# Part of the probabilities in three fp32r passes: a Perceiver layer on one Trainium2 core

## The chip, the core and the metric

The kernel runs on one core of a Trainium2 chip. The metric is the device time of one execution in microseconds (us). TensorE is PE in the profile (PEld its weight loads), VectorE is DVE, ScalarE is ACT, GpSimd is POOL and the DMA queues used are those of SyncE (SP).

## What is computed

One token set of 256 rows of 1024 (x) and a context of 4096 rows go through a cross attention, a linear attention and a mixture of low-rank experts, each with a residual:

```python
x = x + xattn(layernorm(x), ctx)   # 32 heads of 128, 4 key/value heads, keys = context and latents, 4352
x = x + attn(layernorm(x))         # 32 heads, decayed linear attention, RMS norm, sigmoid gate
x = x + ffn(layernorm(x))          # 4 experts of rank 16, top 2
# xattn:
q = latents @ Wq ; k, v = hidden @ Wk, hidden @ Wv
attn = softmax(q @ k.T / sqrt(128))
out = (attn @ v) @ Wo
```

All of it is float32.

## The kernel before

**Precision.** A float32 product is taken in one of two ways. In *three passes* (`three_pass`, line 110) each operand is split into a high part, rounded to fp32r, and a low part, the rest; hi·hi, hi·lo and lo·hi are three fp32r matmuls. *Plain*, a float32 matmul goes to TensorE as it is; the trace shows it as two records.

**Stages.** `project_keys_values` makes keys (high and low, in DRAM) and values (DRAM), and splits the query weights. `cross_attention` follows, then `project_out` with Wo, `linear_attention`, `project_out` again, and `lora_mixture`.

**Cross attention** (line 485) goes over 16 pairs of heads; a pair n is a *slot*, and 512 columns (two heads by 256 tokens). The 4352 keys are 17 double tiles j of 2 x 128. `slots` (line 546) writes the slots' order: slot 0, a loop over three groups of four slots, and three last ones. The key/value head changes every fourth slot, where u is 0. In a slot the engines run side by side, each by its own handwritten order, tied by semaphores:

- TensorE (`pe_slot`, line 903): for each j, the values matmul of pair n (`pe_values`, line 874: probabilities times v, two plain matmuls into `o_ps`), then the scores of pair n+1, two double tiles ahead (`pe_scores`, line 840, six fp32r matmuls). After the last j come the transposes of the maxima (`pe_peak`), the query projection of pair n+3 and the spreading of the maxima over partitions (`pe_spread`).
- VectorE (`dve_slot`, line 790): for each j, the row tile j+1 less the maximum (`dve_shift`, line 771), then the running maximum of pair n+1 (`dve_peak`, lines 746 to 759). In steps 4 to 7 four reciprocals for the previous pair are added (line 779).
- ScalarE (`act_slot`): exp of tile j+1 into one of three buffers of probabilities (`act_exp`, line 646), then the copy of the scores of pair n+1 out of PSUM (`act_row`, line 628).
- GpSimd (`pool_slot`, line 711): the probabilities of tile j are added into `sums` (line 696), 16 additions of 128x1024 a slot, then the two halves to each other (line 702), and in step 9 the previous pair's output is scaled (line 709).

There are three buffers of probabilities, so exp of tile j waits for the values matmul and the addition of tile j-3:

```python
back = j - KEEP
if back >= 0:
    act.wait_ge(pv_done, J * n + back + 1)
    if not last:
        act.wait_ge(added, (J - 1) * n + max(back, 1))
```

In the last slot there are no scores of a next pair. GpSimd adds the odd tiles and VectorE the even ones (line 788), into two tiles that are summed at the end (`pe_sums_last`, line 893). After step 11 VectorE also makes the low parts of the first step of the Wo projection (`Projection.low`, line 977).

**project_out** (line 986) takes 16 steps of two heads, with weights and inputs loaded two steps ahead; the wo instance also loads the first weights of linear attention, in four halves, between its own loads. Then comes a layer norm (`LayerNorm`, line 124): statistics and normalized rows per token tile, transposes by TensorE (line 182), a high part by ScalarE (line 189) and a low part by VectorE (line 195). While TensorE has nothing to do there it runs dummy matmuls (`keep_clock`, line 117), 8 and 10 before the two groups of transposes.

**linear_attention** (line 1221) goes over 16 pairs of heads. Of the two tiles of keys, the second is masked for the first 128 tokens; its scores and values are computed with all 256 columns, and four small tiles of zeros are set by GpSimd at the start.

Of the kernel before, what the change touches and what calls it, by code (L numbers as in the profile page):

```python
# [26 lines left out]
F32R = mybir.dt.float32r  # L27
# [6 lines left out]
KT = HIDDEN // P  # L34
TOK = 256
# [88 lines left out]
class LayerNorm:  # L124
# [53 lines left out]
    def pe_turn(self, pe, t):  # L178

        pe.wait_ge(self.h_ready, t + 1)  # L180
        for k in range(KT):
            last = pe.transpose(self.turned[:, k, t * P:(t + 1) * P], self.h[:, t, k * P:(k + 1) * P], self.ident[:, :])
            if t == QT - 1 and k % 2:
                last.then_inc(self.turned_ready, 1)

    def act_hi(self, act):
        for b in range(KT // 2):
            act.wait_ge(self.turned_ready, b + 1)
            act.activation(self.hT_hi[:, 2 * b:2 * b + 2, :], self.turned[:, 2 * b:2 * b + 2, :],
                           ACT.Copy).then_inc(self.hi_ready, 1)  # L190

    def dve_lo(self, dve):
        for b in range(KT // 2):
            dve.wait_ge(self.hi_ready, b + 1)
            dve.tensor_tensor(self.hT_lo[:, 2 * b:2 * b + 2, :], self.turned[:, 2 * b:2 * b + 2, :],
                              f32(self.hT_hi[:, 2 * b:2 * b + 2, :]), ALU.subtract).then_inc(self.lo_ready, 1)


def project_keys_values(nc, x, ctxT, wk, wv, wq, x_sb, hT_hi, hT_lo, ident, ones, k_drams, v_dram, wq_drams, shared):
# [5 lines left out]
    with ExitStack() as ctx:  # L205
        a = Alloc(nc, ctx, "kv_")
        w_raw = a.sb("w_raw", [P, KT, KVH * D])
# [14 lines left out]
                       k_ps[:, :, :].rearrange("p g (a n) -> p (g a) n", n=TOK), hT_hi, hT_lo, ident)  # L222
# [107 lines left out]
        def _(act):  # L330
# [19 lines left out]
            ln.act_hi(act)  # L350
# [31 lines left out]
        def _(dve):  # L382
# [28 lines left out]
            ln.dve_lo(dve)  # L411
# [25 lines left out]
        def _(pe):  # L437
# [26 lines left out]
            pe.wait_ge(ln.lo_ready, KT // 2)  # L464
# [6 lines left out]
LEAD = 2  # L471
KEEP = 3
# [7 lines left out]
def starts_piece(j):  # L480

    return j == 0 or j in ENDS


def cross_attention(nc, wq_drams, k_drams, v_dram, hT_hi, hT_lo, ident, ones, oT_dram, shared, proj, last_pair):
# [9 lines left out]
    with ExitStack() as ctx:  # L495
        a = Alloc(nc, ctx, "xa_")
        kT_hi, kT_lo = shared.r
        v = a.sb("v", [P, KV])
# [22 lines left out]
        v_in = [a.sem(f"v_in{i}") for i in range(len(ENDS))]  # L521
        q_done = a.sem("q_done")
# [100 lines left out]
        def act_row(act, n, b, j, first=False):  # L623

            act.wait_ge(peak_done, J * n + j + 1)
            if not first:
                act.wait_ge(exp_done, J * (n - 1) + j + 1)
            act.activation(rows[j], s_ps[:, 2 * b:2 * b + 2, :], ACT.Copy).then_inc(row_ready, 1)  # L628

        def act_exp(act, n, j, first=False, last=False):  # L630
# [3 lines left out]
            if back >= 0:  # L634
# [11 lines left out]
            act.activation(probs[j % KEEP], rows[j], ACT.Exp, scale=SCALE).then_inc(exp_done, 1)  # L646

# [49 lines left out]

        def pool_sum(pool, n, first):
# [12 lines left out]
        def pool_slot(pool, n, u, g, first=False, last=False):  # L711
            has_prev, has_next, has_query = flags(u, first, last)
            for j in range(1, J):
                if has_next:
                    pool_add(pool, n, j, not has_prev)
                elif j % 2:
# [4 lines left out]
                    else:  # L721
                        pool.wait_ge(added, (J - 1) * n + j // 2)
# [49 lines left out]

        def dve_inverse(dve, n, c):
# [7 lines left out]
        def dve_add_last(dve, n, j):  # L781

            dve.wait_ge(exp_done, J * n + j + 1)
            if j == 2:
                dve.tensor_copy(peak[:, :, :], probs[j % KEEP]).then_inc(added_last, 1)
            else:
                dve.wait_ge(added_last, j // 2 - 1)
                dve.tensor_tensor(peak[:, :, :], peak[:, :, :], probs[j % KEEP], ALU.add).then_inc(added_last, 1)

        def dve_slot(dve, n, u, g, first=False, last=False):  # L790
            has_prev, has_next, has_query = flags(u, first, last)
            for j in range(J):
                if j + 1 < J:
                    dve_shift(dve, n, j + 1)
                if has_next:
                    dve_peak(dve, n + 1, (u + 1 + j) % 2, j)
                if not has_next and j >= 2 and j % 2 == 0:
# [7 lines left out]
                if not has_next and j == 11:  # L805
# [68 lines left out]
        def pe_values(pe, n, j, values, first):  # L874
# [3 lines left out]
            if values is not None and starts_piece(j):  # L878
                pe.wait_ge(v_in[piece_of(j)], 16 * (values + 1))
            pe.wait_ge(exp_done, J * n + j + 1)  # L880
            for t in range(2):
                at = slice((2 * j + t) * P, (2 * j + t + 1) * P)
                last = pe.matmul(o_ps[:, :], v[:, at], probs[j % KEEP][:, t, :], start=j == 0 and t == 0,  # L883
# [9 lines left out]
        def pe_sums_last(pe):  # L893

            pe.wait_ge(inverse_ready, 4 * LAST + 4)
            pe.wait_ge(added, (J - 1) * LAST + J // 2)
            pe.wait_ge(added_last, J // 2)
# [5 lines left out]
        def pe_slot(pe, n, u, g, first=False, last=False):  # L903
# [7 lines left out]
            for j in range(J):  # L911
                pe_values(pe, n, j, values, not has_prev)
# [31 lines left out]
FIRST_QUARTER = 6  # L944

# [40 lines left out]
def project_out(nc, name, proj, x_sb, h, hT_hi, hT_lo, ident, stores, prefetch, prefetches,  # L986
                norm=None, meanwhile=None, quarters=None, last_pair=None):
# [4 lines left out]
    with ExitStack() as ctx:  # L992
        a = Alloc(nc, ctx, name)
        y_ps = a.ps("y_ps", [P, QT, 2, BANK])
        turned = a.ps("turned", [P, KT, TOK])
# [6 lines left out]
        summed = a.sem("summed")  # L1002
        small = a.sem("small")
        root_ready = a.sem("root_ready")
# [32 lines left out]
        def _(act):  # L1037
# [19 lines left out]
            ln.act_hi(act)  # L1057

        @block.vector
        def _(dve):  # L1060
            proj.low(dve, 1, 1)
            if norm is not None:
                dve.wait_ge(summed, 1)
                dve.tensor_scalar(ve[:, :], turned[:, 0, 0:QT], 1.0 / (HEADS * D), EPS, ALU.mult, ALU.add).then_inc(small, 1)
# [24 lines left out]
            if norm is not None:  # L1089
                dve.wait_ge(small, 6)  # L1090
            for t in range(QT):
                for half in range(2):
# [10 lines left out]
                    if t > 0 and half == 0:  # L1103
# [691 lines left out]
```

## Time and profile before

| | |
|---|---|
| median of 3 runs | 2023.38 us (2022.89 to 2028.67) |
| profiled execution | 2030.37 us, span 2028.5 us |
| mean granted TensorE clock | 0.991 |
| PE busy | 1987.3 us, 98% of the span |
| DVE busy | 1245.9 us, 61% |
| ACT busy | 947.0 us, 47% |
| POOL busy | 776.0 us, 38% |
| cross attention, slots | from about 441 to 1388 us |
| linear attention | 1490 to about 1905 us |

The span is the time from the first to the last instruction; the execution's own time is 1.9 us longer. Busy shares are means over stages with different limits. Weight loads overlap matmuls. A matmul's length in a row includes its way through the array, so the distance between starts, and not the length, is what one costs in a stream.

### The profile page before, as it was taken

The page shows a single profiled execution, that of the slowest core. Times are in us where ns is not written, and L with a number is a line of the kernel's source. Part 1 is how long each engine was busy: PE and PEld are TensorE (multiplying, and loading weights), DVE is VectorE, ACT ScalarE, POOL GpSimd, SP SyncE. Part 2 cuts the span into 40 slices and gives each one's busy share as a digit, 9 for nine tenths or more (in the row PEclk, how much of TensorE's full clock was granted, in tenths as well). Part 3 has the DMA queues.
Part 4 walks back from the last instruction along what each step waited for, and adds up shares of the span by engine and source line. Part 5 has one row for each costly group of instructions (what it writes and reads, how often), then busy time and mean ns, then how long its engine had stood idle before and what let it go on. Part 6 is the DMA issues. An engine that isn't in the chain of part 4 may idle for free. (4 is left out here: it accounts for less than half of the span.)

```text
span 2028.5 us, 27101 instructions
## 1 busy us (share of the span) xinstructions
PE 1987.3 (98%) x9797; PEld 1534.1 (76%) x9797; DVE 1245.9 (61%) x1298; ACT 947.0 (47%) x1000; POOL 776.0 (38%) x345
## 2 busy tenths in 40 slices
PE   9999999999999999999999999998999999999998
PEld 7878888876666666566666666655889999999886
DVE  4312221267877767877677877887756666666555
ACT  3112110155665555665565665654634544445442
POOL 2444320026776666766566766762000000000200
PEclk9999999999999999999999999999999999999998
DMA  8788873420032110321112210015735554444461
GB/s 305 297 310 328 323 280 145 174 93 35 13 109 94 65 48 15 112 92 60 43 47 94 78 60 1 6 57 177 278 136 186 186 184 179 176 176 169 157 233 73
DMA packets 72224, 283.85 MB, mean 140 GB/s; under 512 B 6400, under 2 KB 24320, under 8 KB 56512
## 3 DMA queue, kind: packets, MB, share of 16 engines
q1 hardware_dynamic: 72128, 282.65, 38.1%
q8 instruction: 51, 0.84, 0.2%
q14 instruction: 45, 0.37, 0.1%
HBM read 212.89 MB, written 69.73 MB: 139 GB/s over the span
## 5 line engine op out<-in xcount | busy, mean ns | idle before, releaser
L696 POOL TENSOR_TENSOR xa_sums<-xa_sums,stage 128x1024 f32<-128x1024 f32 x150 | 358.4, 2389 | 117.8 <-ACT stage L646 113.5
L883 PE MATMUL xa_o_ps<-stage,xa_v 128*128 128x512 f32 x768 | 362.3, 595 | 5.4 <-ACT stage L646 5.4
L750 DVE TENSOR_TENSOR xa_peak<-xa_s_ps,xa_peak 128x1024 f32<-128x1024 f32 x224 | 274.1, 1223 | 107.0 <-PE xa_s_ps L114 107.0
L112 PE MATMUL xa_s_ps<-xa_qT_hi,split 128*128 128x512 f32 x544 | 306.9, 564 | 6.6 <-issue 3.9
L628 ACT ACTIVATE xa_rows<-xa_s_ps 128x1024 f32<-128x1024 f32 x208 | 213.4, 1026 | 123.5 <-DVE xa_peak L750 107.4
L771 DVE TENSOR_TENSOR xa_rows<-xa_rows,xa_r_ps 128x1024 f32<-128x1024 f32 x208 | 248.4, 1195 | 0.0
L883 PEld LDWEIGHTS xa_o_ps<-stage,xa_v 128*128 128x128 f32 x768 | 144.2, 190 | 124.3 <-issue 106.2
L114 PE MATMUL xa_s_ps<-xa_qT_hi,split 128*128 128x512 f32 x544 | 215.6, 396 | 0.0
L696 POOL TENSOR_TENSOR xa_sums<-xa_sums,xa_probs 128x1024 f32<-128x1024 f32 x75 | 179.2, 2389 | 91.3 <-ACT xa_probs L646 89.8
L113 PE MATMUL xa_s_ps<-xa_qT_lo,split 128*128 128x512 f32 x544 | 213.5, 392 | 0.0
L646 ACT ACTIVATE stage<-xa_rows 128x1024 f32<-128x1024 f32 x144 | 152.4, 1058 | 100.0 <-DVE xa_rows L771 97.5
L1396 DVE TENSOR_TENSOR pair_lo<-pair_raw,pair_hi 128x4096 fp32r<-128x4096 f32 x30 | 132.8, 4426 | 81.3 <-ACT pair_hi L1333 81.3
L1323 POOL TENSOR_TENSOR square_sum<-square_sum,la_squares 128x512 f32<-128x512 f32 x16 | 20.7, 1295 | 387.5 <-ACT la_squares L1363 387.5
L112 PEld LDWEIGHTS xa_s_ps<-xa_qT_hi,split 128*128 128x128 f32 x544 | 103.2, 190 | 77.2 <-issue 55.8
L373 DVE TENSOR_TENSOR kv_k_lo<-kv_k_ps,kv_k_hi 128x512 fp32r<-128x512 f32 (+1 forms) x36 | 23.5, 660 | 222.2 <-ACT kv_k_hi L321 222.2
L321 ACT ACTIVATE kv_k_hi<-kv_k_ps 128x512 fp32r<-128x512 f32 (+1 forms) x36 | 20.3, 571 | 288.0 <-DMA kT_lo_scratch<-kv_k_lo 228.2
L113 PEld LDWEIGHTS xa_s_ps<-xa_qT_lo,split 128*128 128x128 f32 x544 | 103.4, 190 | 66.9 <-issue 53.6
L883 PE MATMUL xa_o_ps<-xa_probs,xa_v 128*128 128x512 f32 x320 | 150.5, 592 | 1.7 <-ACT xa_probs L646 1.7
L112 PE MATMUL la_qk_ps<-hT_hi,pair_hi 128*128 128x256 f32 x512 | 145.0, 283 | 0.7 <-PEq L992 0.7
L113 PE MATMUL la_qk_ps<-hT_lo,pair_hi 128*128 128x256 f32 x512 | 144.9, 283 | 0.0
L114 PE MATMUL la_qk_ps<-hT_hi,pair_lo 128*128 128x256 f32 x512 | 144.9, 283 | 0.0
L693 POOL TENSOR_TENSOR xa_sums<-stage 128x1024 f32<-128x1024 f32 x15 | 35.9, 2393 | 250.5 <-ACT stage L646 250.5
(301 smaller groups left out, 4672.2 us busy)
## 6 DMA issues: line engine op xcount, KB each, us to landing
pair_raw<-in_w_qk SPq DMA_DIRECT2D x15, 2048.0 KB, 7.7
pair_raw<-in_w_gv SPq DMA_DIRECT2D x15, 2048.0 KB, 7.6
kv_w_raw<-in_wq SPq DMA_DIRECT2D x16, 1024.0 KB, 7.9
wq_hi_scratch<-x_hT_hi SPq DMA_DIRECT2D x16, 1024.0 KB, 4.3
wq_lo_scratch<-x_hT_lo SPq DMA_DIRECT2D x16, 1024.0 KB, 5.0
full<-in_wo SPq DMA_DIRECT2D x16, 1024.0 KB, 5.2
pair_raw<-in_w_out SPq DMA_DIRECT2D x16, 1024.0 KB, 5.0
xa_w_hi<-wq_hi_scratch SPq DMA_DIRECT2D x15, 1024.0 KB, 4.8
```

The source lines that it names most:

```text
L112: pe.matmul(out, w_hi, m_hi, start=first, stop=False)
L113: pe.matmul(out, w_hi, m_lo, start=False, stop=False)
L114: return pe.matmul(out, w_lo, m_hi, start=False, stop=last)
L373: dve.tensor_tensor(k_lo[:, g % 2, 0:n], k_ps[:, g, 0:n], f32(k_hi[:, g % 2, 0:n]), ALU.subtract).then_inc(k_copied, 1)
L628: act.activation(rows[j], s_ps[:, 2 * b:2 * b + 2, :], ACT.Copy).then_inc(row_ready, 1)
L646: act.activation(probs[j % KEEP], rows[j], ACT.Exp, scale=SCALE).then_inc(exp_done, 1)
L693: pool.tensor_tensor(sums[:, :, :], probs[0], probs[1], ALU.add).then_inc(added, 1)
L696: pool.tensor_tensor(sums[:, :, :], sums[:, :, :], probs[j % KEEP], ALU.add).then_inc(added, 1)
L750: dve.tensor_tensor(peak[:, :, :], s_ps[:, 2 * b:2 * b + 2, :], peak[:, :, :], ALU.max).then_inc(peak_done, 1)
L771: dve.tensor_tensor(rows[j], rows[j], r_ps[:, :].unsqueeze(1).to_broadcast([P, 2, W]), ALU.subtract).then_inc(shifted, 1)
L883: last = pe.matmul(o_ps[:, :], v[:, at], probs[j % KEEP][:, t, :], start=j == 0 and t == 0, stop=j == J - 1 and t == 1)
L1396: dve.tensor_tensor(w_lo[part][:, :, :], raw[part][:, :, :], f32(w_hi[part][:, :, :]), ALU.subtract).then_inc(w_lo_ready[part], 1)
```

## The change

Five of the 17 double tiles (j = 2, 5, 8, 11, 14) have their values product in three passes, in all slots but the last. For them ScalarE writes exp a second time, rounded to fp32r (`probs_hi`), and the low part is `probs - probs_hi`: by GpSimd right after its addition for j = 2, 8, 14, by VectorE for j = 5, 11, between the shift of tile j+1 and the maximum. The values of these tiles are split once per key/value head, in slots with u = 0 (ScalarE high, VectorE low, 128x256 each). The last slot is all plain, with the unsplit values of the five tiles loaded into the query weights' buffer; its additions go 12 to GpSimd and 4 to VectorE, and the low parts of the first Wo step come after the last tile. Values are loaded in 12 pieces instead of 4.

To make room, `x_sb` lives only from the Wo projection on and x is loaded twice. Layer norms turn and split one token tile after the other, the last parts of the out projection are reordered so that token tile 0 is complete earlier, and the dummy matmuls are 1 and 13. In linear attention the masked half of the second key tile is left out: 128 columns instead of 256, and no zeros are set.

```diff
+SPLIT_STEPS = (2, 5, 8, 11, 14)
+LOW_BY_VECTOR = (5, 11)
+LAST_BY_VECTOR = (4, 8, 12, 16)
...
             act.activation(probs[j % KEEP], rows[j], ACT.Exp, scale=SCALE).then_inc(exp_done, 1)
+            if j in SPLIT_STEPS and not last:
+                act.activation(probs_hi[:, :, :], rows[j], ACT.Exp, scale=SCALE).then_inc(probs_hi_ready, 1)
...
+                if u == 0 and j + 2 in SPLIT_STEPS:
+                    act_values(act, g, j + 2)
...
+        def pool_low(pool, n, j):
+
+            pool.wait_ge(exp_done, J * n + j + 1)
+            pool.wait_ge(probs_hi_ready, SPLIT * n + SPLIT_STEPS.index(j) + 1)
+            pool.tensor_tensor(probs_lo[:, :, :], probs[j % KEEP], f32(probs_hi[:, :, :]), ALU.subtract).then_inc(low_by_pool, 1)
...
                 if has_next:
                     pool_add(pool, n, j, not has_prev)
+                    if j in LOW_BY_POOL:
+                        pool_low(pool, n, j)
...
                 if j + 1 < J:
                     dve_shift(dve, n, j + 1)
+                if has_next and j in LOW_BY_VECTOR:
+                    dve_low(dve, n, j)
                 if has_next:
                     dve_peak(dve, n + 1, (u + 1 + j) % 2, j)
+                if u == 0 and j + 2 in SPLIT_STEPS:
+                    dve_values(dve, g, j + 2)
...
-                if not has_next and j == 11:
+                if not has_next and j == J - 1:
                     proj.low(dve, 0, 0)
...
+            if j in SPLIT_STEPS and not last_slot:
+                if values is not None:
+                    pe.wait_ge(v_lo_ready, SPLIT * values + SPLIT_STEPS.index(j) + 1)
+                if j in LOW_BY_VECTOR:
+                    pe.wait_ge(low_by_vector, len(LOW_BY_VECTOR) * n + LOW_BY_VECTOR.index(j) + 1)
+                else:
+                    pe.wait_ge(low_by_pool, len(LOW_BY_POOL) * n + LOW_BY_POOL.index(j) + 1)
+                for t in range(2):
+                    at = slice(split_columns(j).start + t * P, split_columns(j).start + (t + 1) * P)
+                    last = three_pass(pe, o_ps[:, :], v_hi[:, at], v_lo[:, at], probs_hi[:, t, :], probs_lo[:, t, :],
+                                      False, False)
...
+LAST_PARTS = ((0, 0, 0), (0, 0, 1), (0, 1, 0), (1, 0, 0), (1, 0, 1), (0, 1, 1), (1, 1, 0), (1, 1, 1))
...
-            for t, count in zip(range(QT), (8, 10)):
+            for t, count in zip(range(QT), (1, 13)):
...
-                    last = three_pass(pe, a_ps[:, h, jt, :], qk_hi[:, h, 1, key], qk_lo[:, h, 1, key],
-                                      qk_hi[:, h, 0, :], qk_lo[:, h, 0, :], True, True)
+                    at = slice(jt * P, TOK)
+                    last = three_pass(pe, a_ps[:, h, jt, at], qk_hi[:, h, 1, key], qk_lo[:, h, 1, key],
+                                      qk_hi[:, h, 0, at], qk_lo[:, h, 0, at], True, True)
...
         def load_first_pair(sp, i):
+            if i == 3:
+                sp.dma_start(x_sb[:, :, :], x).then_inc(x_in, 16)
             weights.load_half(sp, i // 2, i % 2)
```

## Rows read from the trace of the kernel before

**Rows 1.** Stretches: us, PE, PEld, DVE, ACT, POOL busy, clock, DMA share, GB/s.
```profile
808.38:869.09 60.71, 60.71 (x235) 39.36 (x234) 46.74 (x43) 36.40 (x36) 40.70 (x19) 1.00 0.33 113
1346.20:1388.10 41.90, 34.82 (x81) 14.65 (x80) 38.02 (x32) 20.76 (x21) 21.65 (x9) 0.96 0.19 69
1490.00:1895.00 405.00, 405.00 (x3376) 405.00 (x3376) 242.31 (x274) 197.44 (x216) 20.33 (x20) 1.00 0.49 179
```

**Rows 2.** Timeline of TensorE, one step: start us, us, engine, line, what.
```profile
811.13 1.88 PE L883 MATMUL xa_o_ps<-stage,xa_v 128*128 128x512 f32 x4
813.08 0.40 PE L113 MATMUL xa_s_ps<-xa_qT_lo,split 128*128 128x512 f32 x1
814.24 1.88 PE L883 MATMUL xa_o_ps<-stage,xa_v 128*128 128x512 f32 x4
```

**Rows 3.** GpSimd and TensorE at tile 2; GpSimd subtractions at L982 (min/median/max ns).
```profile
813.65 2.39 POOL L696 TENSOR_TENSOR xa_sums<-xa_sums,xa_probs 128x1024 f32<-128x1024 f32 x1 [4.02 <-ACT xa_probs L646]
816.12 4.86 POOL L696 TENSOR_TENSOR xa_sums<-xa_sums,stage 128x1024 f32<-128x1024 f32 x2
817.34 1.88 PE L883 MATMUL xa_o_ps<-xa_probs,xa_v 128*128 128x512 f32 x4
L982 POOL TENSOR_TENSOR pair_hi<-pair_raw,pair_hi x2: 2399/2402/2406, 1896.6 to 1899.0; 128x1024 fp32r<-128x1024 f32 x2
```

**Rows 4.** ScalarE and TensorE: exp and values of tile 8.
```profile
830.98 1.06 ACT L646 ACTIVATE xa_probs<-xa_rows 128x1024 f32<-128x1024 f32 x1 [0.99 <-DVE xa_rows L771]
836.81 1.88 PE L883 MATMUL xa_o_ps<-xa_probs,xa_v 128*128 128x512 f32 x4
```

**Rows 5.** VectorE in steps 6 and 7 of the same slot.
```profile
827.70 1.22 DVE L750 TENSOR_TENSOR xa_peak<-xa_s_ps,xa_peak 128x1024 f32<-128x1024 f32 x1
828.85 0.95 DVE L779 RECIPROCAL xa_inverse<-xa_t_ps 128x128 f32<-128x128 f32 x1
829.71 1.16 DVE L771 TENSOR_TENSOR xa_rows<-xa_rows,xa_r_ps 128x1024 f32<-128x1024 f32 x1
```

**Rows 6.** VectorE and GpSimd, last slot; lines 982 and 753 (min/median/max ns).
```profile
1373.62 4.50 DVE L982 TENSOR_TENSOR split<-full,split 128x1024 fp32r<-128x1024 f32 x2
1374.13 2.90 POOL L723 TENSOR_TENSOR xa_sums<-xa_sums,xa_probs 128x1024 f32<-128x1024 f32 x1 [1.03 <-ACT xa_probs L646]
L982 DVE TENSOR_TENSOR split<-full,split x16: 1211/1223/3362, 1373.6 to 1466.3; 128x1024 fp32r<-128x1024 f32 x16
L753 DVE TENSOR_TENSOR xa_peak<-xa_peak x16: 692/2254/2259, 426.8 to 1338.1; 128x512 f32<-128x512 f32 x16
```

**Rows 7.** Last slot: GpSimd's first addition and TensorE's closing sums.
```profile
1351.40 2.35 POOL L720 TENSOR_TENSOR xa_sums<-stage 128x1024 f32<-128x1024 f32 x1 [5.20 <-ACT stage L646]
1387.96 1.45 PE L900 MATMUL xa_t_ps<-xa_sums,ones 128*128 128x512 f32 x3
```

**Rows 8.** TensorE: transposes in the first stage, then the spreading of the maxima.
```profile
345.87 1.91 PE L182 MATMUL kv_k_ps<-ident,kv_w_raw 128*128 128x128 f32 x16
347.53 0.48 PE L112 MATMUL kv_v_ps<-kv_wv_hi,kv_c_hi 128*128 128x512 f32 x1
863.17 1.05 PE L870 MATMUL xa_r_ps<-ident,xa_max_q 128*128 128x128 f32 x8
863.98 0.36 PE L112 MATMUL xa_q_ps<-x_hT_hi,xa_w_hi 128*128 128x256 f32 x1
```

**Rows 9.** Timeline of the tail after the first out projection.
```profile
1479.68 1.98 PE L121 MATMUL wo_y_ps<-wo_odd 128*128 128x512 f32 x8
1487.01 2.48 DVE L195 TENSOR_TENSOR hT_lo<-wo_turned,hT_hi 128x512 fp32r<-128x512 f32 x4 [1.16 <-ACT hT_hi L189]
1489.81 0.36 PE L112 MATMUL la_qk_ps<-hT_hi,pair_hi 128*128 128x256 f32 x1 [0.73 <-PEq L992]
```

**Rows 10.** Busy time by stretch: the first out projection, ten us.
```profile
1430.00:1440.00 10.00, 10.00 (x45) 8.27 (x45) 7.50 (x8) 6.96 (x8) 0.00 (x0) 1.00 0.95 356
```

More of the change, by code:

```diff
@@ L34 @@
 KT = HIDDEN // P
+HALF = KT // 2
 TOK = 256
@@ L349, in _ @@
             act.wait_ge(wq_stored, 32 * (PAIRS + 1))
-            ln.act_hi(act)
+            for t in range(QT):
+                ln.act_hi(act, t)
             copy_keys(act, NCHUNK, TOK)
@@ L410, in _ @@
             copy_values(dve, NCHUNK - 1, 1)
-            ln.dve_lo(dve)
+            for t in range(QT):
+                ln.dve_lo(dve, t)
             copy_values(dve, NCHUNK - 1, VT, 1)
@@ L471 @@
 LEAD = 2
+LAST_BY_VECTOR = (4, 8, 12, 16)
+LAST_BY_POOL = tuple(j for j in range(1, J) if j not in LAST_BY_VECTOR)
+SPLIT_STEPS = (2, 5, 8, 11, 14)
+LOW_BY_VECTOR = (5, 11)
+LOW_BY_POOL = tuple(j for j in SPLIT_STEPS if j not in LOW_BY_VECTOR)
+SPLIT = len(SPLIT_STEPS)
 KEEP = 3
@@ L482, in starts_piece, with plain_columns, split_columns, value_runs @@
     return j == 0 or j in ENDS
+def plain_columns(j0, j1):
+    back = sum(s < j0 for s in SPLIT_STEPS)
+    return slice(2 * P * (j0 - back), 2 * P * (j1 - back))
+def split_columns(j):
+    i = SPLIT_STEPS.index(j)
+    return slice(2 * P * i, 2 * P * (i + 1))
+def value_runs(i):
+    runs, start = [], ENDS[i - 1] if i else 0
+    for j in range(start, ENDS[i]):
+        if j in SPLIT_STEPS:
+            if start < j:
+                runs.append((start, j))
+            runs.append((j, j + 1))
+            start = j + 1
+    if start < ENDS[i]:
+        runs.append((start, ENDS[i]))
+    return runs
 def cross_attention(nc, wq_drams, k_drams, v_dram, hT_hi, hT_lo, ident, ones, oT_dram, shared, proj, last_pair):
@@ L584, in sync_slot @@
                 load_weight(sp, n + 3)
+            if last and u == 2:
+                sp.wait_ge(q_done, PAIRS)
+                load_last_values(sp)
             if not has_next:
@@ L872, in pe_spread, with pe_values @@
             last.then_inc(spread, 1)
-        def pe_values(pe, n, j, values, first):
+        def pe_values(pe, n, j, values, first, last_slot):
             if j == 0 and not first:
@@ L911, in pe_slot @@
             for j in range(J):
-                pe_values(pe, n, j, values, not has_prev)
+                pe_values(pe, n, j, values, not has_prev, not has_next)
                 if has_next and j + LEAD < J:
@@ L1001, in project_out @@
         r0 = a.sb("r0", [P, QT])
-        summed = a.sem("summed")
-        small = a.sem("small")
-        root_ready = a.sem("root_ready")
+        if norm is not None:
+            summed = a.sem("summed")
+            small = a.sem("small")
+            root_ready = a.sem("root_ready")
         mm_done = a.sem("mm_done")
@@ L1090, in _ @@
                 dve.wait_ge(small, 6)
+            if x_in is not None:
+                dve.wait_ge(x_in, 16)
             for t in range(QT):
@@ L1102, in _ @@
                     ln.dve_stats(dve, t, half)
-                    if t > 0 and half == 0:
-                        ln.dve_rows(dve, t - 1)
                 ln.dve_variance(dve, t)
-            ln.dve_rows(dve, QT - 1)
-            ln.dve_lo(dve)
+                ln.dve_rows(dve, t)
+            for t in range(QT):
+                ln.dve_lo(dve, t)
         def part(pe, par, h, t, b, first, last):
@@ L1128, in _ @@
                     for h in range(2):
-                        last = pe.matmul(turned[:, 0, t:t + 1], square_sum[:, h, t * P:(t + 1) * P], ones[:, 0:1],
+                        last = pe.matmul(turned[:, 0, 0, t:t + 1], square_sum[:, h, t * P:(t + 1) * P], ones[:, 0:1],
                                          start=h == 0, stop=h == 1)
```

143 lines of the change are left out of this document (91 added, 52 removed).

## The prediction

> **What bounds the kernel now.** I read the busy time by stretch first. In one slot of cross attention (808.38 to 869.09, the fifteen slots with a successor repeat it) TensorE is busy 60.71 of 60.71 us with the granted clock at full (2.4 GHz), while VectorE has 46.74, ScalarE 36.40 and GpSimd 40.70 us of work. The last slot, 41.90 us, is the one stretch of this part where TensorE has gaps. Linear attention, 405.00 us, is TensorE without a gap too [rows 1]. Then the timeline of TensorE inside the slot: a step is 811.13 to 814.24, 3.11 us. The second scores matmul starts at 813.08 and one such matmul is 0.23 us, so the plain values of a double tile take 811.13 to 812.85, 1.72 us, and the six fp32r scores matmuls 1.39 us [rows 2]. Third, the clearance between an exp and the values that use it, on the timelines of ScalarE, GpSimd and TensorE [rows 3, 4]; what a faster TensorE would collide with stands there.
>
> **The gain that is bought.** Six fp32r matmuls of 128x512 in place of four plain records: 1.72 - 1.39 = 0.33 us per split tile [rows 2], 1.65 us per slot, 75 tiles, 24.8 us in all, if nothing waits. ScalarE gets a second exp of 1.06 us five times a slot (5.3 us on top of 36.4): no bound by itself.
>
> **Tile 2.** GpSimd's addition of it starts at 813.65, released by its exp, and GpSimd's next instruction at 816.12, that and its successor lasting 4.86: back to back these are 2.44 us apart [rows 3]. The next one is now the subtraction, of the shape of the GpSimd fp32r subtraction of 128x1024, 2.40 us [rows 3]. It ends at about 818.5, and TensorE wants tile 2 at 817.34 [rows 3]. That exp hangs on the slot's first scores, so nothing moves it forward: TensorE waits 1.3 us with the hand-over, in each of fifteen slots.
>
> **Tile 8.** Its exp runs from 830.98 to 832.04 and TensorE takes it at 836.81: 4.8 us clear [rows 4]. Addition plus subtraction want 2 x 2.44 = 4.9 us, with hand-overs a wait of 0.3 us already with nothing late. But it will be late. In steps 4 to 7 VectorE runs peak, reciprocal and shift back to back: 827.70, 828.85, 829.71, next peak 3.1 us after the first, all of TensorE's step [rows 5]. The subtraction of tile 5 (1.22 us) is put there.
>
> It also meets the thing I take as this change's main price: a VectorE instruction with both inputs in SBUF and a GpSimd instruction don't run together. In the last slot two subtractions of 1.22 us each last 4.50 us from 1373.62, and GpSimd's addition from 1374.13 lasts 2.90 instead of 2.39: first it waits for VectorE's first one, then VectorE's second waits for it. The 128x512 maximum of two SBUF halves at line 753 takes 0.69 us at best and 2.25 in the median of the 16 slots [rows 6]. Instructions with one input in PSUM (the peak, the shift) keep their time beside GpSimd [rows 5]. The Trainium skill says the same (SBUF, State Buffer, "Who interferes with whom": a VectorE instruction with two SBUF inputs contends with a GpSimd instruction that reads SBUF, and one is fully blocked); by that rule the trace agrees. So tile 5's subtraction waits 1.1 us for an addition that is under way, takes 1.2, and GpSimd's next addition starts some 0.9 us later.
>
> Walking it through, in time from the slot's start (808.38): TensorE takes tile 2 at 10.25, not 8.96, and ends scores 4 at 13.0. VectorE does peak 4 from 13.2 (1.14 us), reciprocal (0.86) and shift 6 (1.13) to 16.3. GpSimd has ended tile 2's subtraction at 10.1 and adds tiles 3, 4, 5 until 17.45; tile 5's subtraction on VectorE waits for that and ends at 18.6. Peak 5, reciprocal, shift 7 (3.13), peak 6, reciprocal (2.0): shift 8 starts at 23.75, before at 829.71 - 808.38 = 21.3 [rows 5]. Exp 8 ends 2.4 us after it (1.27 to its start, as 829.71 to 830.98, and 1.06), 26.15; its addition runs 26.3 to 28.7, its subtraction to 31.15. TensorE could have taken tile 8 at 29.1 (28.43 before, +1.3, -0.66). It waits 2.15 us.
>
> **Tile 14.** From 26.3 on GpSimd does not rest: seven additions (8 to 14), two subtractions, the output of the previous pair (1.25), and VectorE's blocking instructions between them (tile 11, 1.2; line 753, 0.6): 9 x 2.44 + 3.05 = 25.0, so the low part of tile 14 is there at 51.3. TensorE would want it at 49.3: another 2.05 us.
>
> **Sum per slot:** waits 1.3 + 2.15 + 2.05 = 5.5, gain 1.65, net +3.85. Fourteen slots make +53.9; the first has no reciprocals and no output, so I give it +1.5. Bounds: above, GpSimd's two idle stretches (2.2 and 0.7 us before additions 7 and 8 in this walk) are in it already, so little more than +5. Below, without those stretches and without any blocking: GpSimd's chain from tile 2 to 14 is 16 x 2.44 + 1.25 = 40.3 from 5.27, tile 14 at 45.6, before TensorE needs it, and only tile 2 and 0.3 at tile 8 are left: 1.6 - 1.65 = -0.05.
>
> **Values split once per four slots.** Five small VectorE subtractions of 128x256 (about 0.35 us, from 1.22 for 1024) with both inputs in SBUF: each may wait up to 2.4 us for GpSimd, most of them where VectorE has 0.7 us a step to spare. I take +1.3 in each of four slots, +5 (0 to +12).
>
> **Last slot.** All plain. Additions go 12 to GpSimd, 4 to VectorE (before 8 and 8), and they exclude each other: 12 x 2.43 + 4 x 1.2 + 1.3 = 35.3 us from 1351.40 [rows 7]. That ends at 1386.7, where the closing sums start at 1387.96 now [rows 7]. The wo subtractions no longer hold a shift (that wait is gone), but the additions take its place. -0.5 (-4 to +3).
>
> **Linear attention.** 192 matmuls go from 256 to 128 columns. At 256 one takes 405.00/3376 = 0.120 us [rows 1]. No row has fp32r with 128. Lower end: half the columns off, 0.120 - 0.053 = 0.067, so -10. Upper end: a plain fp32 product of 128 columns is two records, eight of them from 863.17 to 863.98, so 0.20 us and +16 [rows 8]. Nearest: transposes of 128x128, each with its own weights, 16 from 345.87 to 347.53, 0.104 us each [rows 8]; I take that, -3. The Trainium skill (TensorE: Matmul & The Clock Gate, "LDWEIGHTS (loading the stationary operand)") gives a load as its columns over 1.2 GHz, 107 ns for 128; by it the term would be -2.5, and by the sustained 81 ns of "Back-to-back issue gap" -7.5. The four memsets that go were on idle GpSimd: 0.
>
> **Layer norms.** After each out projection the tail is 1479.68 to 1489.81, 10.1 us, and the last of it four low pieces, 2.48 us [rows 9]. With token tile 0 turned and split first only two pieces are left (-1.2), and the reordered last parts let tile 1's row start about 0.3 us earlier: -1.5 each, two tails, -3 (-5 to 0). The dummies before the transposes, 1 and 13 instead of 8 and 10, fill the same gap. In the first stage the turned tiles are covered by value matmuls: 0. The second load of x, 1 MB, (3 us at 356 GB/s) joins DMA engines that are 0.95 busy, but TensorE is busy 10.00 of 10.00 us there [rows 10]: 0 (to +3). Eight more load issues of values on SP's queue lie beside a whole slot: 0.
>
> **Total:** 53.9 + 1.5 + 5 - 0.5 - 3 - 3 = +53.9. The profiled execution took 2030.4 us (span 2028.5), so 2084; the median of the runs is 2023.4, and 2023.4 + 53.9 = 2077.
>
> **Rivals.**
> (A) Faster: GpSimd keeps up. The place is the pair of waits at tiles 8 and 14. For it speaks that GpSimd has 20 us free in a slot and that exp 8 led by 4.8 us [rows 1, 4]; against it the full VectorE steps and the blocking [rows 5, 6]. It decides when the waits of a slot stay under 1.65 us. With tile 2 alone waiting: 15 x -0.35 = -5, last slot, linear attention and norms -6.5, split values +1: -11, 2012.
> (B) The light version: blocking delays only a little, tile 8 waits 0.9, tile 14 0.6, net +1.15 a slot: +17 - 1.5 = 2039.
> (C) Narrow fp32r falls to the plain price: forecast + 19, 2096.
> (D) The waits come to 1.75 us a slot, +1.5 in all, against the other terms' -1.5: 2023, no change.
> (E) That the five tiles would stay plain in effect: outside the last slot the code sends all five through three passes, so this gets no chance.
>
> **How the numbers follow.** Forecast 0.60, (B) 0.16, (C) 0.08, (A) 0.10, (D) 0.06. A change under 0.3%, 6 us, can't be told from none here. Slower 0.84, same 0.06, faster 0.10. The range goes from (B)'s lower side, 2032, to between the forecast's upper bounds and (C), 2099.
>
> **What the profile after would show.** Right: the low-part subtraction on GpSimd about 2.4 us, TensorE idle before the fp32r values of tiles 2, 8 and 14, released by GpSimd, some 75 to 80 us in all; slots near 64.5 us; VectorE's subtraction at tiles 5 and 11 lasting over 2 us in the mean. Wrong: slots at or under 60.7 us, GpSimd with rests after tile 8, or TensorE released by ScalarE instead.

## The result, and the profile after

| | before | after |
|---|---|---|
| median | 2025.22 us (4 runs, 2022.89 to 2028.67) | 2084.59 us (4 runs, 2082.53 to 2096.87) |
| profiled execution, span | 2030.37, 2028.5 us | 2082.53, 2080.8 us |
| ratio | | 1.030, 95% interval 1.027 to 1.034: slower |

The page of the changed kernel, busy time of the engines:

```profile
PE 1970.9 (95%) x9939; PEld 1548.3 (74%) x9939; DVE 1305.4 (63%) x1344; ACT 1010.7 (49%) x1095; POOL 918.4 (44%) x390
```

Between the medians the change costs 59.4 us, between the two profiled executions 52.2 us; the stretches below are of these two executions.

TensorE is busy 16 us less than before, and its share falls from 98 to 95%: it has less to do and waits. The busy time by stretch (us, PE, PEld, DVE, ACT, POOL busy, clock, DMA share, GB/s) of an ordinary slot, two slots with u = 0 (the longest and another), the last slot and linear attention, in the changed kernel:

```profile
891.05:954.59 63.54, 59.92 (x244) 40.88 (x243) 48.70 (x45) 40.49 (x42) 49.57 (x22) 1.00 0.24 82
690.56:762.12 71.56, 63.14 (x243) 42.41 (x243) 57.27 (x50) 41.31 (x47) 48.83 (x22) 0.95 0.12 43
1215.39:1283.33 67.94, 60.41 (x244) 40.72 (x243) 55.39 (x50) 41.10 (x47) 49.48 (x22) 1.00 0.13 45
1405.84:1451.79 45.95, 39.66 (x96) 17.15 (x95) 36.15 (x29) 22.82 (x25) 32.89 (x15) 0.96 0.18 63
1548.79:1960.65 411.86, 411.23 (x3445) 411.06 (x3445) 248.07 (x283) 202.37 (x225) 26.05 (x19) 1.00 0.49 179
```

The first row stands against the 60.71 us of [rows 1], in which TensorE had no gap. Slots are cut here at the four transposes of the maxima, which stand once in each; the kernel before cut in the same way gives the middle column (differences of start times on the timelines of TensorE):

| stretch | before | after | difference |
|---|---|---|---|
| up to the first transposes of maxima | 431.07 | 431.61 | +0.54 |
| eight slots with u = 1, 2 or 3 | 60.67 to 60.72 | 63.54 to 63.61 | +2.84 to +2.94 each |
| four slots with u = 0 | 61.29, 60.70, 60.70, 60.70 | 68.18, 71.56, 67.90, 67.94 | +6.89, +10.86, +7.20, +7.24 |
| two slots after a turn of the loop | 64.40, 64.70 | 65.38, 65.78 | +0.98, +1.08 |
| all 15 to the last transposes | 913.48 | 974.23 | +60.75 |
| last slot, to the first Wo matmul | 47.94 | 45.95 | -1.99 |
| Wo projection and its norm | 97.32 | 97.00 | -0.32 |
| linear attention, to its last product | 414.13 | 411.86 | -2.27 |
| second projection and norm | 107.08 | 105.35 | -1.73 |
| mixture, to the end | 17.48 | 14.80 | -2.68 |

(The slot of 58.96 us that closes the 15, against 55.41, projects no query; it is the one not listed, +3.55.) The loss is wholly in the slots. What TensorE waits for there, from the waits of the changed kernel (total us, times, longest):

```profile
PE xa_o_ps L113 <- POOL xa_probs_lo L777: 56.9, 45, 1.8
PE xa_s_ps L113 <- ACT xa_rows L693: 14.3, 8, 3.2
```

The first is three tiles in 15 slots. One ordinary slot on the timeline of TensorE (start us, us, engine, line, what, idle before): the values of tiles 2, 8 and 14, and the matmul ahead of the last wait.

```profile
909.95 0.50 PE L113 MATMUL xa_o_ps<-xa_probs_hi,xa_v_hi 128*128 128x512 f32 x1 [0.94 <-POOL xa_probs_lo L777]
...
930.51 0.50 PE L113 MATMUL xa_o_ps<-xa_probs_hi,xa_v_hi 128*128 128x512 f32 x1 [1.37 <-POOL xa_probs_lo L777]
...
948.28 0.40 PE L115 MATMUL xa_s_ps<-xa_qT_hi,split 128*128 128x512 f32 x1
949.99 0.50 PE L113 MATMUL xa_o_ps<-xa_probs_hi,xa_v_hi 128*128 128x512 f32 x1 [1.31 <-POOL xa_probs_lo L777]
950.33 0.40 PE L114 MATMUL xa_o_ps<-xa_probs_lo,xa_v_hi 128*128 128x512 f32 x1
```

A stall costs more than its idle time: matmuls in a stream start 0.23 us apart, so the one at 949.99 could have started at 948.51, 1.48 us earlier and not 1.31, and the next one follows it after 0.34 us. That is 1.6 us for 1.31 shown, so about 0.29 us more at each stall.

GpSimd in the same slot, from tile 2 to tile 14, and VectorE's subtraction of tile 5:

```profile
905.16 2.38 POOL L771 TENSOR_TENSOR xa_sums<-xa_sums,xa_probs 128x1024 f32<-128x1024 f32 x1 [4.02 <-ACT xa_probs L711]
907.51 2.38 POOL L777 TENSOR_TENSOR xa_probs_lo<-xa_probs,xa_probs_hi 128x1024 fp32r<-128x1024 f32 x1
909.86 4.85 POOL L771 TENSOR_TENSOR xa_sums<-xa_sums,stage 128x1024 f32<-128x1024 f32 x2
...
916.08 2.18 DVE L860 TENSOR_TENSOR xa_probs_lo<-xa_probs,xa_probs_hi 128x1024 fp32r<-128x1024 f32 x1
917.49 3.05 POOL L771 TENSOR_TENSOR xa_sums<-xa_sums,stage 128x1024 f32<-128x1024 f32 x1 [0.32 <-ACT stage L711]
...
925.74 2.37 POOL L771 TENSOR_TENSOR xa_sums<-xa_sums,xa_probs 128x1024 f32<-128x1024 f32 x1 [0.69 <-ACT xa_probs L711]
928.08 2.37 POOL L777 TENSOR_TENSOR xa_probs_lo<-xa_probs,xa_probs_hi 128x1024 fp32r<-128x1024 f32 x1
...
936.49 3.25 POOL L771 TENSOR_TENSOR xa_sums<-xa_sums,xa_probs 128x1024 f32<-128x1024 f32 x1
...
947.10 2.84 POOL L777 TENSOR_TENSOR xa_probs_lo<-xa_probs,xa_probs_hi 128x1024 fp32r<-128x1024 f32 x1
```

The low part comes behind the addition at 905.16 and 925.74, and from 925.74 to 949.9 no row carries a wait: 24.2 us without rest. The addition of 3.05 us is held by VectorE's subtraction of tile 5, that of 3.25 by tile 11's (from 935.83, 1.67 us), and the low part of 2.84 us starts beside the 128x512 maximum of two SBUF halves (946.87). VectorE's subtractions by line (860 probabilities, 866 values; min/median/max ns):

```profile
L860 DVE TENSOR_TENSOR xa_probs_lo<-xa_probs,xa_probs_hi x30: 1266/1800/2536, 457.6 to 1386.9; 128x1024 fp32r<-128x1024 f32 x30
L866 DVE TENSOR_TENSOR xa_v_lo<-xa_v_lo,xa_v_hi x20: 412/1988/2483, 443.1 to 1269.8; 128x256 fp32r<-128x256 f32 x20
```

The second row is the one I had not taken seriously enough. Where it happens, step 6 of the slot with u = 0 that takes 71.56 us (VectorE, GpSimd and ScalarE):

```profile
723.30 2.38 POOL L771 TENSOR_TENSOR xa_sums<-xa_sums,stage 128x1024 f32<-128x1024 f32 x1 [2.15 <-ACT stage L711]
...
723.48 2.48 DVE L866 TENSOR_TENSOR xa_v_lo<-xa_v_lo,xa_v_hi 128x256 fp32r<-128x256 f32 x1 [0.38 <-ACT xa_v_hi L719]
...
725.88 0.94 DVE L874 RECIPROCAL xa_inverse<-xa_t_ps 128x128 f32<-128x128 f32 x1
...
728.02 1.06 ACT L711 ACTIVATE xa_probs<-xa_rows 128x1024 f32<-128x1024 f32 x1 [3.66 <-DVE xa_rows L854]
...
730.98 0.50 PE L113 MATMUL xa_s_ps<-xa_qT_hi,split 128*128 128x512 f32 x1 [3.20 <-ACT xa_rows L693]
```

A subtraction of 128x256 starts 0.18 us behind a GpSimd addition and ends with it, 2.48 us later, in a step in which VectorE has nothing to spare. All maxima, shifts and exps behind it move back. ScalarE makes the copy of the scores after the exp in its order, so the copy is late too, and in the end TensorE waits 3.20 us for it: a wait of another name than the 45, in none of my terms.

The slot is 3.6 us longer than the two like it (67.90 and 67.94 us), and that is the clock. All three have this wait, 3.20, 3.19 and 3.20 us; their mean granted clocks are 0.95, 0.97 and 1.00. Behind the wait at 730.98 TensorE ran at 1.2 GHz: the fp32r matmuls from 735.02 to 738.86 start 0.43 us apart instead of 0.23 (granted clock 0.53 from 732 to 739 us). VectorE's shifts lie at the same places of this slot and of the one of 67.94 us up to 46 us after its start, and 3.6 us later at its end.

### The profile page after: what moved, and what is told of

Its sections match the earlier page's. It is cut to its first block and busy times, and to the rows that moved or that the text cites. A ratio compares the mean times of both kernels' runs of the same rounds, so it can differ in the third digit from the quotient of the medians.

```text
span 2080.8 us, 27859 instructions
## 1 busy us (share of the span) xinstructions
PE 1970.9 (95%) x9939; PEld 1548.3 (74%) x9939; DVE 1305.4 (63%) x1344; ACT 1010.7 (49%) x1095; POOL 918.4 (44%) x390
## 5 line engine op out<-in xcount | busy, mean ns | idle before, releaser
L771 POOL TENSOR_TENSOR xa_sums<-xa_sums,stage 128x1024 f32<-128x1024 f32 x150 | 368.3, 2455 | 45.0 <-ACT stage L711 39.5
L113 PE MATMUL xa_s_ps<-xa_qT_hi,split 128*128 128x512 f32 x544 | 269.5, 495 | 20.0 <-ACT xa_rows L693 14.3
L771 POOL TENSOR_TENSOR xa_sums<-xa_sums,xa_probs 128x1024 f32<-128x1024 f32 x75 | 190.0, 2533 | 88.7 <-ACT xa_probs L711 85.2
L115 PE MATMUL xa_s_ps<-xa_qT_hi,split 128*128 128x512 f32 x544 | 214.6, 394 | 0.0
L1440 POOL TENSOR_TENSOR square_sum<-square_sum,la_squares 128x512 f32<-128x512 f32 x16 | 20.8, 1301 | 385.7 <-ACT la_squares L1480 385.7
L113 PEld LDWEIGHTS xa_s_ps<-xa_qT_hi,split 128*128 128x128 f32 x544 | 102.7, 189 | 89.6 <-ACT xa_rows L693 34.9
L115 PEld LDWEIGHTS xa_s_ps<-xa_qT_hi,split 128*128 128x128 f32 x544 | 102.6, 189 | 23.4
```

The lines of the kernel that those rows point to most:

```text
L113: pe.matmul(out, w_hi, m_hi, start=first, stop=False)
L115: return pe.matmul(out, w_lo, m_hi, start=False, stop=last)
L771: pool.tensor_tensor(sums[:, :, :], sums[:, :, :], probs[j % KEEP], ALU.add).then_inc(added, 1)
```

## Experiments

Each is an edit of the changed kernel unless it says otherwise. The time of before beside them was 2024.8 to 2026.7 us.

**1. No tile split.**

```diff
-SPLIT_STEPS = (2, 5, 8, 11, 14)
-LOW_BY_VECTOR = (5, 11)
+SPLIT_STEPS = ()
+LOW_BY_VECTOR = ()
```

> The changed kernel with no tile in three passes (the list of split tiles is empty; no second exp, no low parts, no split values), all its other parts kept: last slot 12 to 4, layer norms, 128 columns in linear attention, second load of x. Theory: the whole loss is in the slots. TensorE's maxima transposes lie 60.75 us further apart from the first to the last in the changed kernel than before, and everything outside gives about -8.5 us; so the slots go back to 60.70 us and the time is about 2016 us (2013 to 2020), ratio to before 0.9955. Rival: one of the other parts costs something that the slots hide (the second load of x, the reordered last parts), and the time is 2022 us or more.

2018.5 us (6 runs), ratio 0.9965 (0.9953 to 0.9977). An ordinary slot, by stretch:

```profile
858.82:919.54 60.72, 60.72 (x234) 39.37 (x233) 46.74 (x43) 36.43 (x37) 40.68 (x19) 1.00 0.24 86
```

The ordinary slots are those of before, and the other parts together gain some 7 us. All of the loss is the splitting.

**2. The values' subtraction with an input from PSUM.** VectorE has an instruction of the same size, on other numbers: the values' low parts are not computed.

```diff
-            dve.tensor_tensor(v_lo[:, at], f32(v_lo[:, at]), f32(v_hi[:, at]), ALU.subtract)
+            dve.tensor_tensor(v_lo[:, at], f32(v_lo[:, at]), r_ps[:, 0:2 * P], ALU.subtract)
```

> The changed kernel, but VectorE's subtraction for the values of a split tile (128x256) takes its second input from a tile in PSUM instead of the high part in SBUF; same size, same waits, so the values' low parts are not the right ones. Theory (blocking): in the slots with u = 0 this instruction took 1.75 us in the mean instead of 0.35 because GpSimd was adding, and that cost these four slots 4.0 to 8.0 us each beyond the others, some 21 us in all; with one input in PSUM they fall to within 1 us of the other slots (63.6): about 2066 us (2063 to 2072), ratio to the changed kernel 0.991. Rival (the work itself, ScalarE's copies and the twelve loads delay these slots): less than 4 us saved, 2081 us or more.

2067.9 us (4 runs), ratio to before 1.0207 (1.0190 to 1.0224), 16.7 us less than the changed kernel. By line and form the instruction is now

```profile
L866 DVE TENSOR_TENSOR xa_v_lo<-xa_v_lo,xa_r_ps 128x256 fp32r<-128x256 f32 x20 | 8.4, 419 | 5.8 <-ACT xa_v_hi L719 5.8
```

419 ns in place of 1751. The slots with u = 0 are 65.05, 64.70, 64.72 and 64.69 us, the others as they were (63.6). With an instruction of the same size, 1.1 us a slot is left of the 4 to 8. The blocking made the rest: 3.2 us in three of the slots and 6.9 in the one of 71.56, where 3.6 of them are the fall of the clock behind the wait, which is not there in this run.

**3. The same for VectorE's low parts of tiles 5 and 11**, which are then not computed either.

```diff
-            dve.tensor_tensor(probs_lo[:, :, :], probs[j % KEEP], f32(probs_hi[:, :, :]), ALU.subtract)
+            dve.tensor_tensor(probs_lo[:, :, :], probs[j % KEEP], r_ps[:, :].unsqueeze(1).to_broadcast([P, 2, W]),
+                              ALU.subtract)
```

> The changed kernel, but VectorE's low parts of tiles 5 and 11 (128x1024) take their second input from PSUM (the spread maxima) instead of the high part; same size and waits, so these low parts are not the right ones. Theory (blocking): the subtraction of tile 5 falls from 2.18 to 1.22 us, shift and exp of tile 8 come 0.96 us earlier and TensorE's wait at tile 8 falls from 1.37 to 0.4; GpSimd's addition beside tile 11's subtraction falls from 3.25 to 2.4 us and the wait at tile 14 from 1.31 to about 0.45. 1.8 us a slot, about 2057 us (2050 to 2064). Rival (GpSimd's amount of work sets both waits, not the blocking): the slots stay over 63 us and the time over 2077 us.

2048.5 us (4 runs), ratio to before 1.0120 (1.0104 to 1.0137). The instruction by line, and tile 8 on TensorE:

```profile
L860 DVE TENSOR_TENSOR xa_probs_lo<-xa_probs,xa_r_ps x30: 1203/1209/1216, 457.2 to 1350.6; 128x1024 fp32r<-128x1024 f32 x30
909.93 0.50 PE L113 MATMUL xa_o_ps<-xa_probs_hi,xa_v_hi 128*128 128x512 f32 x1 [0.61 <-POOL xa_probs_lo L777]
```

Ordinary slots are 61.3 us, 2.2 less (I had 1.8): the wait at tile 8 falls from 1.37 to 0.61, at tile 14 it is gone, at tile 2 it stays 0.94. The slots with u = 0 are still 66.0 us (the first 67.4). What VectorE's subtraction loses to GpSimd counts twice, once as a later exp 8 and once as a longer addition in GpSimd's own list. The time is 1.5 us under the range that I gave.

**4. The low part before the addition** on GpSimd, nothing left out.

```diff
-                    pool_add(pool, n, j, not has_prev)
                     if j in LOW_BY_POOL:
                         pool_low(pool, n, j)
+                    pool_add(pool, n, j, not has_prev)
```

> The changed kernel, but GpSimd makes the low part of tiles 2, 8 and 14 before it adds the tile. Theory (backlog): the waits at tiles 2 and 8 go, since the low part comes up to 2.4 us earlier, but GpSimd still runs back to back from exp 8 to tile 14 (24.3 us in the changed kernel, less the addition of 14 = 21.9 us, and now it starts a second exp later), so its low part comes about 47.5 us after the slot's first values, TensorE wants it at 45.6, and tile 14 still waits 1.5 to 2 us: slots near 61 us, about 2045 us (2038 to 2050). Rival (only the order at each tile matters): all three waits go, the slots are 60.70 - 1.85 = 58.85 us and the time is 2014 to 2022 us.

2028.1 us (10 runs), ratio to before 1.0014 (1.0005 to 1.0023): 56 us for the exchange of two instructions. GpSimd at tiles 8 and 14:

```profile
895.08 2.40 POOL L777 TENSOR_TENSOR xa_probs_lo<-xa_probs,xa_probs_hi 128x1024 fp32r<-128x1024 f32 x1 [1.14 <-ACT xa_probs_hi L713]
897.43 2.43 POOL L771 TENSOR_TENSOR xa_sums<-xa_sums,xa_probs 128x1024 f32<-128x1024 f32 x1
...
914.30 2.83 POOL L777 TENSOR_TENSOR xa_probs_lo<-xa_probs,xa_probs_hi 128x1024 fp32r<-128x1024 f32 x1
```

The ordinary slots are 60.80 us and TensorE waits at tile 14 alone, 1.4 to 1.5 us: the mechanism and the slot are the theory's. The time, 10 us under my range, is not, since I forgot the slots with u = 0 in the sum: with the slack won they fall from some 68 (one 71.56) to 62.3 us (the first to 62.9), and VectorE's values subtraction from 1751 to 743 ns in the mean.

**5. The stretch from exp 8 to tile 14 made shorter**: experiment 4, with the scaling of the output behind tile 14's low part.

```diff
-                if has_prev and j == 9:
+                if has_prev and j == (15 if has_next else 9):
                     pool_output(pool, n - 1, 1 - u % 2, 8 * (n - u % 2) + 16)
```

> The kernel with the low part ahead of the addition on GpSimd (only tile 14 waits, a stall of 1.75 us a slot), with the scaling of the previous pair's output (1.3 us on GpSimd) moved from step 9 to step 15, behind tile 14's low part; complete. Theory (between exp 8 and tile 14 GpSimd does not rest, so each microsecond taken from that stretch comes off the wait): the stall falls to about 0.45 us, the slots to 59.5 us in 14 slots, 2010 us (2006 to 2015). Rival (the wait hangs on exp 14 and not on GpSimd's list): no change, 2026 to 2030 us. A later output also holds the store and the key and value loads behind it on SP's queue; if these were needed sooner, the slots with a new key/value head would be longer by over 2 us.

2009.1 us (4 runs), ratio 0.9923 (0.9902 to 0.9944). No wait at tile 14 is left: 1.73 us went with its hand-over, for 1.3 us of GpSimd's work. Ordinary slots are 59.40 us, only 1.40 less, because 0.33 us is lost in a new place. The scores behind tile 11's values wait for their copy, and two matmuls there start 0.43 and 0.34 us after the one before them instead of 0.23; VectorE's subtraction of tile 11 just ahead takes 2.99 us.

**6. Tile 14 not split**, with experiment 4 (`SPLIT_STEPS = (2, 5, 8, 11)`).

> GpSimd's low part ahead of its addition, and tile 14 not split: four split tiles (2, 5, 8, 11); complete. Theory (backlog): the wait at tile 14 is gone with nothing in its place, the slots are 60.70 - 4 x 0.37 = 59.2 us, 2004 us (2000 to 2009). Rival (the wait came from something ahead of tile 14, and goes to an exp near it): slots at 60.5 us or more, 2020 us or more.

2005.5 us (4 runs), ratio 0.9903 (0.9888 to 0.9918). Ordinary slots 59.40 us, no wait for a low part.

**7. Tile 14's low part by VectorE**, with experiment 4 (`LOW_BY_VECTOR = (5, 11, 14)`).

> The changed kernel with GpSimd's low part ahead of its addition, and tile 14's low part given to VectorE (as tiles 5 and 11 have it); complete. In the run with the low part first, only the wait at tile 14 was left (1.45 us and its hand-over) and the slots were 60.80 us. Theory (GpSimd's backlog from exp 8 to tile 14 is the last cost): one low part less and no one waiting for it, no wait is left, the slots are 60.70 - 5 x 0.37 = 58.85 us, 1999 us (1995 to 2005), faster than the kernel before. Rival (VectorE's third subtraction, near 1.8 us with the blocking, delays the last maxima or the rows of the slot's end): slots at 60 us or more, 2015 us or more.

2012.1 us (6 runs), ratio 0.9938 (0.9921 to 0.9954). Ordinary slots are 59.03 to 59.31 us, near the theory's, but the slots with u = 0 are 62.8 us (the first 63.7): there TensorE waits 0.97 and 0.6 us for rows and 1.2 us for the last maxima. The rival's mechanism was right in these slots, and I had again left them out of the sum; the time lies between the two ranges.

**8. As 7, with the values' low parts on GpSimd too.**

```diff
+                    if u == 0 and j + 1 in SPLIT_STEPS:
+                        pool_values(pool, g, j + 1)
                     pool_add(pool, n, j, not has_prev)
...
-                if u == 0 and j + 2 in SPLIT_STEPS:
-                    dve_values(dve, g, j + 2)
```

> As the kernel with the low part first and tile 14 on VectorE, but GpSimd also makes the low parts of the values (128x256, ahead of its addition, one step before the tile), so VectorE has none; complete. Theory (blocking of VectorE in its full steps is what the slots with u = 0 paid): their 1.5 us each beyond the others go, another 4 to 6 us off, 1994 us (1990 to 2000). Rival (GpSimd has no room for them in its backlog, or the loads bind): no change or slower than the kernel without this.

2001.9 us (5 runs, 1999.4 to 2005.3), ratio 0.9884 (0.9868 to 0.9899), 10 us less than 7. The time is 1.9 us over my range. The slots with u = 0 are 60.9 us and not 59.1; in three of them 1.1 us is a wait for the last maxima. An ordinary one, by stretch:

```profile
849.71:908.78 59.07, 59.07 (x244) 41.08 (x243) 50.09 (x46) 40.19 (x42) 48.59 (x21) 1.00 0.26 88
```

TensorE has no gap again, and a slot is 60.70 - 59.07 = 1.63 us shorter than before. This kernel leaves nothing out and takes 1.2% less time than the kernel before.

**9. As 6, with the values' low parts on GpSimd.**

> Four split tiles (2, 5, 8, 11), the low part ahead of the addition, and the low parts of the values on GpSimd; complete. Theory: the slots with u = 0 (60.78 us with the values' low parts on VectorE, the others 59.40) come to within 0.5 us of the others, 2001 us (1997 to 2005), so the fifth tile is worth little. Rival (GpSimd's four additional instructions bring back a wait at tile 11 or 8 in these slots): 2005 us or more.

2003.6 us (4 runs), ratio 0.9898 (0.9881 to 0.9915). The slots with u = 0 are 59.99 us, the others 59.4 to 59.5. It can't be told from 8: the fifth tile's 0.33 us a slot is about what it costs in the slots with u = 0.

**10. No tile split, 8 and 10 dummies.**

```diff
-            for t, count in zip(range(QT), (1, 13)):
+            for t, count in zip(range(QT), (8, 10)):
```

> The kernel without split tiles, with 8 and 10 dummy matmuls around the transposes of the layer norms as before, instead of 1 and 13. Before, the granted clock was 0.50 for the first 5 us of the mixture stage; in the changed kernel it is 1.00 there and this stage is 2.4 us shorter. Theory (the shorter gap ahead of it, from turning and splitting one token tile after the other): the clock stays at 1.00 there, the time within 1 us of the kernel without split tiles. Rival (the 13 dummies behind the transposes of token tile 0 keep it up): the clock is 0.5 again for some us of that stage and it is some 2 us longer.

2022.8 us (one run), which can't be told from experiment 1 (2016.7 to 2022.5). This one shows that my question was a wrong one. The first 5 us of the mixture in four kernels, by stretch: before; after; experiment 1; experiment 10.

```profile
2011.00:2016.00 5.00, 4.98 (x24) 4.98 (x24) 0.24 (x7) 1.48 (x2) 0.00 (x0) 0.50 0.02 5
```

```profile
2066.00:2071.00 5.00, 4.53 (x32) 3.78 (x33) 1.29 (x15) 2.31 (x5) 0.00 (x0) 1.00 0.00 0
```

```profile
2002.35:2007.35 5.00, 5.00 (x24) 4.96 (x24) 0.27 (x7) 1.45 (x2) 0.00 (x0) 0.50 0.02 5
```

```profile
2004.23:2009.23 5.00, 4.53 (x27) 4.12 (x27) 0.27 (x7) 1.84 (x3) 0.00 (x0) 0.66 0.01 2
```

Experiment 1 has the changed kernel's norms and dummies and yet runs at 0.50, and 8 and 10 dummies run at 0.66: neither theory stands. The 2.7 us that the mixture gained in the profile of after are not shown to be the change's.

## Why the prediction was right, and which terms were not

The sign, the place and the sum were right: 2077 (2032 to 2099) predicted, 2084.6 measured; +53.9 us forecast, 2082.5 - 2030.4 = +52.2 between the two profiled executions and +59.4 between the medians. By terms the sum is less good than it looks. For the 15 slots it had +60.4 us, and +60.75 were measured; but the stalls were 12.6 us too high in it, the split of the values 15.8 us too low, and 3.6 us of clock at the turns of the loop came back without a term. That these cancel is luck.

Of the signs it named, the low part of 2.4 us and the waits at tiles 2, 8 and 14 are there; their sum is 56.9 us and not 75 to 80, the slots are 63.55 and not 64.5, and VectorE's subtraction of tiles 5 and 11 lasts 1.91 us in the mean and not over 2.

- **The gain per tile, 0.33 us: right.** Without a stall an ordinary slot of five split tiles takes 59.07 us (experiment 8) and of four 59.40 (6), so a tile is worth 0.33. In the changed kernel 1.65 was earned and 4.50 paid: 60.70 - 1.65 + 4.50 = 63.55.
- **Tile 2, 1.3 us: right.** 0.94 of idle time and 0.29 of hand-over, 1.23. The low part ended at 909.9, 10.0 us after the slot's start (899.9, 2.75 us ahead of the second values as in [rows 2]); I had 10.1.
- **Tile 8, 2.15 us: mechanism right, size 1.66.** The shift of tile 8 began 23.4 us into the slot (23.75 in my walk) and the low part ended at 30.6 (31.15). The blocking of tile 5's subtraction was 2.18 - 1.22 = 0.96 us where I had 1.1, and addition and low part took 4.71 us (4.85). Experiment 3 shows that the blocking is in it: without it the wait is 0.61 in place of 1.37.
- **Tile 14, 2.05 us: mechanism right, size 1.60.** GpSimd ran 24.2 us without rest (25.0 in the prediction). Experiments 3, 5, 6 and 7 each took something out of this stretch (or the tile, in 6), and each time the wait went.
- **Sum per slot, +3.85: 2.85 measured.** For the 15 slots the prediction's 53.9 + 1.5 stands against 15 x 2.85 = 42.8. The missing 1 us a slot is the size of the two stalls above; the bound below (-0.05, no blocking at all) was far off and is excluded by experiment 3, whose slots without the blocking of tiles 5 and 11 still take 61.3.
- **Values split, +5 (0 to +12): wrong, about +21, outside its bounds.** The four slots with u = 0 lose 32.2 us, and at 2.85 each for the rest of the mechanism 20.8 are theirs; without the 3.6 us of the clock in one of them it is 17, still outside. The price of the instruction was right as a bound ("up to 2.4 us": 2.48 at most, 1.75 in the mean; unblocked it takes 0.42, for the 0.35 expected). The step that failed is "most of them where VectorE has 0.7 us a step to spare". Tile 8's values come in step 6, among the reciprocals, where the prediction's own walk leaves VectorE no slack; there the subtraction took 2.38 to 2.48 us, and in three of the four slots the wait of 3.2 us follows. These waits stay (2.94 to 2.97 us) in experiment 3, so the blocking of tile 5's low part does not make them. Experiment 2 takes 16.7 us back.
- **The turn of the loop: no term, -3.6 us.** TensorE stands 1.86 us there before, and after that the clock was down for some us (0.79 in the mean of 744 to 752 us); in the changed kernel it stood 1.47 us and the clock stayed at 1.00. Experiment 1, whose slots are those of before, has 62.75 and 64.71 us at the two turns: without and with the dip in one execution. So the 3.6 us are not shown to be the change's.
- **Last slot, -0.5 (-4 to +3): -2.0.** Of TensorE's waits, the one of 2.58 us, right behind the subtractions of [rows 6], fell to 0.60, and those of 2.56, 1.38 and 0.94 stayed. GpSimd's longer list did bind, by 0.44 us: its last addition, 3.14 us long, ends at 1447.08, and TensorE, idle since 1446.74, starts the closing sums at 1447.18. Before, there was no gap.
- **Linear attention, -3 (-10 to +16): -2.3**, 12 ns for each of 192 narrow matmuls. The Trainium skill's weight-load figure (TensorE: Matmul & The Clock Gate, "LDWEIGHTS (loading the stationary operand)"), by which the term was estimated at -2.5, came nearest; its sustained figure of 81 ns ("Back-to-back issue gap"), -7.5, did not hold here.
- **Layer norms, -3: -2.1.** From the last matmul of the Wo projection to linear attention it is 8.9 us where it was 10.4, the -1.5 of the prediction, and behind the second projection 8.6 where it was 10.6. But the first projection itself takes 1.1 us longer; among this is a wait of 0.50 us for a low part, new, which all ten experiments have as well, at 0.35 to 0.65. Whether the second load of x ahead of its inputs does that was not tried.

Rivals (A) and (D) fell at the waits of tiles 8 and 14, (B) at their size, (C) at linear attention.

## What to carry to other kernels

Where one engine gets a second task for the same tile, put the one that the critical engine waits for first: here two instructions in the other order were worth 56 us of 2084.6. A short VectorE instruction with both inputs in SBUF cost here what was left of GpSimd's instruction (up to 2.48 us for 0.42), so it belongs on GpSimd itself or in a step with slack for that. Price rare slots by themselves: what four of fifteen slots lost beyond the others was a third of the slots' loss.

## What the runs showed of the hardware

- A VectorE subtraction of 128x256 took 1751 ns in the mean beside GpSimd with both inputs in SBUF and 419 with one of them in PSUM; one of 128x1024, 1.8 us in the median and 1209 ns. GpSimd's instruction of 128x256 took 741 ns in the median of experiment 8, and 1.7 us in six of twenty. The Trainium skill states the rule (SBUF, State Buffer, "Who interferes with whom"); that it makes the short instruction the expensive one is this trace's.
- A stall of TensorE shown as 1.31 us cost 1.6.
- The same code ran at 1.2 or at 2.4 GHz for some microseconds behind the same gap. At the first turn of the loop TensorE stood 1.86 us before and the clock fell, and 1.78 us in experiment 1 and it did not; of three waits of 3.2 us in one execution the slots' mean clocks were 0.95, 0.97 and 1.00. Differences of 2 to 4 us between single executions can be that alone.
- A narrow fp32r matmul gains little. The four scores products of linear attention (two with 256 columns, two with 128), then the next 256:

```profile
1881.17 0.28 PE L113 MATMUL la_a_ps<-split 128*128 128x256 f32 x1
...
1881.53 0.22 PE L113 MATMUL la_a_ps<-split 128*128 128x128 f32 x1
1881.59 0.28 PE L114 MATMUL la_a_ps<-split 128*128 128x128 f32 x1
1881.71 0.27 PE L115 MATMUL la_a_ps<-split 128*128 128x128 f32 x1
1881.82 0.33 PE L113 MATMUL la_a_ps<-split 128*128 128x256 f32 x1
...
1882.51 0.33 PE L113 MATMUL la_qk_ps<-hT_hi,pair_hi 128*128 128x256 f32 x1
```

Twelve matmuls take 1.34 us, against 12 x 0.120 = 1.44 with 256 columns throughout [rows 1]: half of the columns off six of them brings 0.10 us.
